# Probabilities times context values of two sequences in one product of full width, with separate instruction orders for the opening and the closing step

## The reference, cut to what matters

```python
def _L0_xattn_ref(Q, K, V, mask, Wq, Wk, Wv, Wo):
    B, S, E = Q.shape                 # 64, 64, 128
    H, Dk = (N_HEAD, D_K)             # 16, 8
    q = (Q @ Wq.T).reshape(B, S, H, Dk).transpose(0, 2, 1, 3)
    k = (K @ Wk.T).reshape(B, S, H, Dk).transpose(0, 2, 1, 3)
    v = (V @ Wv.T).reshape(B, S, H, Dk).transpose(0, 2, 1, 3)
    scores = jnp.einsum('bhqd,bhkd->bhqk', q, k) / jnp.sqrt(jnp.float32(Dk))
    attn = jax.nn.softmax(scores, axis=-1)
    ctx = jnp.einsum('bhqk,bhkd->bhqd', attn, v)
    ctx = ctx.transpose(0, 2, 1, 3).reshape(B, S, E)
    return ctx @ Wo.T
...
    x = x + _L0_attn_ref(_layernorm(x, axis=-1), ...)
    x = x + _L0_xattn_ref(_layernorm(x, axis=-1), ctx_1024, ctx_1024, mask_1_bf0, ...)
    x = x + _L0_ffn_ref(_layernorm(x, axis=-1), ...)
```

## Time and profile before

| | us |
|---|---|
| median of 3 runs | 347.01 |
| lowest, highest | 342.46, 348.94 |
| the profiled execution, its time | 346.9 |
| the profiled execution, span of its instructions | 345.1 |
| TensorE busy (share of the span) | 298.0 (86%) |
| TensorE weight loads busy | 214.0 (62%) |
| VectorE busy | 238.8 (69%) |
| ScalarE busy | 238.0 (69%) |
| GpSimd busy | 168.9 (49%) |

### The profile page before, as it was taken

How to read it: one execution, slowest core, us unless ns; L and a number is a source line. 1 busy time by engine, 2 the same in 40 slices (tenths; PEclk the granted TensorE clock), 3 DMA queues, 4 the chain that set the end, 5 groups by cost and what they waited for, 6 DMA issues and landing times.

```text
span 345.1 us, 9523 instructions
## 1 busy us (share of the span) xinstructions
PE 298.0 (86%) x3666; PEld 214.0 (62%) x3666; DVE 238.8 (69%) x549; ACT 238.0 (69%) x399; POOL 168.9 (49%) x210
## 2 busy tenths in 40 slices
PE   6546886999999999999999999999989988889851
PEld 6343776755866586658665866586658645745640
DVE  3764286686788788878887878787875585334546
ACT  6692744589958995899589958995898476216602
POOL 5359129225655396539653964375437531230220
PEclk9995589899999999999999999999999999659995
DMA  3901001100210011002200020012001100100011
GB/s 91 264 19 31 20 0 32 48 0 8 66 41 3 7 50 25 3 6 61 75 2 8 22 53 2 9 42 63 1 8 48 26 3 2 30 2 2 2 30 30
DMA packets 15948, 10.64 MB, mean 31 GB/s; under 512 B 2848, under 2 KB 14112, under 8 KB 15904
## 3 DMA queue, kind: packets, MB, share of 16 engines
q1 hardware_dynamic: 15648, 9.91, 10.7%
q10 hardware_dynamic: 256, 0.13, 0.2%
HBM read 4.79 MB, written 2.10 MB: 20 GB/s over the span
## 4 chain that ended last, share of the span: by engine, by line
PE 60%; ACT 14%; DVE 12%; issue 8%; ACTq 2%; SPq 2%; DMA 1%; POOL 1%; POOLq 0%; DVEq 0%
PE AT L675 10%; PE S L748 7%; PE PT L781 6%; PE PB L800 4%; PE PA L692 4%; DVE at L1380 3%; ACT pr L1118 3%; DVE nmax L1432 3%; PE S L761 3%; PE PB L813 2%; PE PA L708 2%; ACT prT L1123 2%; ACT L1089 2%; ACT L1044 2%; PE PT L580 2%
## 5 line engine op out<-in xcount | busy, mean ns | idle before, releaser
L1432 DVE TENSOR_REDUCE nmax<-S 128x16 bf16<-128x1024 f32 x30 | 36.7, 1223 | 14.9 <-PE S L748 14.9
L675 PE MATMUL AT<-q_bd,kc 128*64 128x128 f32 x512 | 36.4, 301 | 8.4 <-DVE at L1380 4.3
L800 PEld LDWEIGHTS PB<-v_x,prT 128*64 128x64 f32 x960 | 32.3, 139 | 18.0 <-ACT prT L1123 13.2
L675 PEld LDWEIGHTS AT<-q_bd,kc 128*64 128x64 f32 x512 | 32.3, 152 | 17.2 <-issue 15.1
L1123 ACT COPY prT<-PT 128x512 f32<-128x512 f32 x60 | 34.8, 580 | 11.6 <-PE PT L781 9.6
L781 PE MATMUL PT<-ident,pr 128*128 128x128 f32 x240 | 38.3, 282 | 2.5 <-ACT pr L1118 1.3
L1008 ACT ACTIVATE k_bd<-S,k_rows 128x512 f32<-128x512 f32 x64 | 39.7, 691 | 0.7 <-DVE k_rows L1541 0.7
L781 PEld LDWEIGHTS PT<-ident,pr 128*128 128x128 f32 x240 | 26.0, 140 | 22.6 <-issue 11.6
L1118 ACT ACTIVATE pr<-S,rs 128x1024 f32<-128x1024 f32 x30 | 33.4, 1115 | 9.0 <-PE S L761 9.0
L800 PE MATMUL PB<-v_x,prT 128*64 128x18 f32 x960 | 36.9, 214 | 2.9 <-ACT prT L1123 2.9
L453 POOL TENSOR_TENSOR kc<-ke,e_r 128x512 f32<-128x512 f32 x32 | 36.0, 1143 | 0.6
(11 more groups left out here) (170 smaller groups left out, 681.9 us busy)
## 6 DMA issues: line engine op xcount, KB each, us to landing
cT<-in_ctxT SPq DMA_DIRECT2D x8, 256.0 KB, 3.4
v_bd<-vt SPq DMA_DIRECT2D x32, 64.0 KB, 2.1
out<-yout SPq DMA_DIRECT2D x8, 256.0 KB, 2.2
q_bd<-qs SPq DMA_DIRECT2D x112, 8.0 KB
x_all<-in_x SPq DMA_DIRECT2D x2, 256.0 KB, 3.4
q_bd<-qs ACTq DMA_DIRECT2D x16, 8.0 KB
wv_s<-in_wv SPq DMA_DIRECT2D x1, 64.0 KB, 2.0
wg_s<-in_wg SPq DMA_DIRECT2D x1, 64.0 KB, 1.9
```

Source lines behind the costliest of these rows:

```text
L675: last = nc.tensor.matmul(AT[L * w:L * w + L, c * NB * CH:(c + 1) * NB * CH], kc_m[:, i, c, :], q_bdv[:, :, L * i + CH * c:L * i + CH * c ...
L800: last = nc.tensor.matmul(dst[L * half:L * half + L, 2 * VC * p:2 * VC * p + 2 * VC], prT_v[:, p, L * half:L * half + L], v_xv[:, g % 2, 2 ...
L1432: nc.vector.tensor_reduce(nmax[:, XH * (i % 2):XH * (i % 2) + XH], cut(s_buf(g, i), XH, L), AX.X, ALU.max, negate=True).then_inc(s_max, 1)
```

## The change

The change has two parts.

The product. `x_values` now takes all 128 columns of a block of `prT` as weights, and the values of both sequences of the tile, 2 x 18 columns, as the moving side. Every token is thus multiplied with the values of its own sequence and with those of the other one. `cx` is twice as large (`x` = 0 or 1 says with whose values). `b_weigh` takes the sums of the first part alone, since the ones are the same in both, and multiplies both parts. `x_out` no longer transposes with a transposition: for each tile and each sequence it is a product with 128 columns of `cx` as weights and 64 columns of the identity moving, which transposes and takes, of the part x, only the tokens of sequence x.

The orders. Step 0 and step 6 have lists of their own (`opening`, `closing`), `step` serves 1 to 5, and the lists of all engines are written in another order, SP's too. `keep_awake` gets more places: in `first` 14 parts before the first scores of cross attention, where there were 9, three inside `closing`, one at the start of `last` as before, three before the last transposition, where there were two. In the last group they wait for `s_og`, for they write to PA0.

```diff
@@
-        cx, cxT, x2 = sb("cx", GT), sb("cxT", GT), sb("x2", GT)
+        cx, cxT, x2 = sb("cx", 2 * GT), sb("cxT", GT), sb("x2", GT)
+        cx_v = cut(cx, TPG, 2, E)
...
@@
-        def run(first, step, last):
+        def run(first, opening, step, closing, last):
 
             first()
-            for n in range(NG - 1):
+            opening()
+            for n in range(1, NG - 2):
                 step(n)
+            closing()
             last()
...
@@
                 dst = pv_buf(g, i)
+                both = dst[:, 0:2 * XH * VC].rearrange("p (x q v) -> p x q v", x=2, q=PAIRS)
                 for p in range(hp * n, hp * n + hp):
-                    for half in range(2):
-                        last = nc.tensor.matmul(dst[L * half:L * half + L, 2 * VC * p:2 * VC * p + 2 * VC],
-                                                prT_v[:, p, L * half:L * half + L], v_xv[:, g % 2, 2 * i + half, p, :],
-                                                start=True, stop=True)
+                    last = nc.tensor.matmul(both[:, :, p, :], prT_v[:, p, :], v_xv[:, g % 2, 2 * i:2 * i + 2, p, :],
+                                            start=True, stop=True)
                 last.then_inc(s_PV, 1)
 
             def x_out(g):
                 pe.wait_ge(s_cx, TPG * g + TPG)
                 pe.wait_ge(s_prT, 2 * TPG * (g + 1))
-                to_features(PT, cx).then_inc(s_CX, 1)
+                for i in range(TPG):
+                    for half in range(2):
+                        at_c = P * i + L * half
+                        last = nc.tensor.matmul(PT[:, at_c:at_c + L], cx_v[:, i, half, :],
+                                                ident[:, L * half:L * half + L], start=True, stop=True)
+                last.then_inc(s_CX, 1)
...
@@
             def keep_awake(g, part):
-                if part >= AWAKE:
+                if g == NG - 1:
+                    pe.wait_ge(s_og, NG)
+                elif part >= AWAKE:
                     pe.wait_ge(s_WC, 1)
...
@@
                 dve.wait_ge(s_PV, 2 * (TPG * g + i) + 2)
-                pv = pv_buf(g, i)[:, 0:XH * VC].rearrange("p (h v) -> p h v", h=XH)
+                pv = pv_buf(g, i)[:, 0:2 * XH * VC].rearrange("p (x h v) -> p x h v", x=2, h=XH)
                 mine = rden[:, XH * (i % 2):XH * (i % 2) + XH].unsqueeze(2)
-                nc.vector.reciprocal(mine, pv[:, :, XD:VC]).then_inc(s_rden, 1)
+                nc.vector.reciprocal(mine, pv[:, 0, :, XD:VC]).then_inc(s_rden, 1)
                 dve.wait_ge(s_rden, TPG * g + i + 1)
                 if i == 0:
                     dve.wait_ge(s_CX, g)
-                nc.vector.tensor_tensor(cx[:, E * i:E * i + E].rearrange("p (h v) -> p h v", h=XH), pv[:, :, 0:XD],
-                                        mine.to_broadcast([P, XH, XD]),
+                nc.vector.tensor_tensor(cx_v[:, i, :, :].rearrange("p x (h v) -> p x h v", h=XH), pv[:, :, :, 0:XD],
+                                        mine.unsqueeze(1).to_broadcast([P, 2, XH, XD]),
                                         ALU.mult).then_inc(s_cx, 1)
```

More of the change, by code:

```diff
@@ L321, in last @@
                 pass
-            run(first, step, last)
+            run(first, opening, step, closing, last)
             sp.wait_ge(s_out, 16 * NG)
@@ L537, in step @@
+                group_norm(b)
+                route2(c)
+                spans(a)
+                count(c)
+                products(a)
                 if has(a + 2):
                     scale_a(a + 2)
[L539 to L549, removed]
@@ L886, in first, with opening @@
                 scores(1, 1)
+                x_scores(0, 0)
+            def opening():
                 attend(1, 0, 0)
+                attend(1, 0, 1)
+                attend(1, 1, 0)
+                less_max(0, 0)
+                project_qk(2)
+                x_scores(0, 1)
+                x_attend(0, 0, 0)
+                attend(1, 1, 1)
+                less_max(0, 1)
+                project_g(2)
+                x_attend(0, 0, 1)
+                x_scores(0, 2)
+                less_max(0, 2)
+                x_values(0, 0, 0)
+                x_values(0, 0, 1)
+                project_v(2)
+                x_scores(0, 3)
+                x_attend(0, 1, 0)
+                transpose_o(1)
+                x_attend(0, 1, 1)
+                x_values(0, 1, 0)
+                aug_weights(2)
+                x_values(0, 1, 1)
+                x_attend(0, 2, 0)
+                less_max(0, 3)
+                x_attend(0, 2, 1)
+                transpose_x(3)
+                context_keys(2)
+                x_values(0, 2, 0)
+                x_values(0, 2, 1)
+                x_attend(0, 3, 0)
+                gla_out(1)
+                x_attend(0, 3, 1)
+                x_values(0, 3, 0)
+                x_values(0, 3, 1)
+                context_values(2)
+                x_out(0)
+                scores(2, 0)
+                x_out2(0)
+                queries(1)
+                scores(2, 1)
+                queries2(1)
+                attend(2, 0, 0)
             def step(n):
@@ L941, in step, with closing @@
                 x_out2(n)
[L942 to L944 removed]
+                scores(a, 0)
                 queries2(b)
[L946 to L948 removed]
+                scores(a, 1)
+                attend(a, 0, 0)
+            def closing():
+                attend(7, 0, 1)
+                x_scores(6, 0)
+                transpose_x2(5)
+                attend(7, 1, 0)
+                attend(7, 1, 1)
+                less_max(6, 0)
+                router(5)
+                ffn(5)
+                x_attend(6, 0, 0)
+                x_scores(6, 1)
+                x_attend(6, 0, 1)
+                x_values(6, 0, 0)
+                less_max(6, 1)
+                x_scores(6, 2)
+                x_attend(6, 1, 0)
+                x_values(6, 0, 1)
+                less_max(6, 2)
+                x_attend(6, 1, 1)
+                x_values(6, 1, 0)
+                x_scores(6, 3)
+                transpose_o(7)
+                x_values(6, 1, 1)
+                x_attend(6, 2, 0)
+                less_max(6, 3)
+                x_attend(6, 2, 1)
+                x_values(6, 2, 0)
+                gla_out(7)
+                x_attend(6, 3, 0)
+                x_values(6, 2, 1)
+                x_attend(6, 3, 1)
+                x_values(6, 3, 0)
+                x_values(6, 3, 1)
+                keep_awake(7, 23)
+                x_out(6)
+                keep_awake(7, 21)
+                x_out2(6)
+                queries(7)
+                keep_awake(7, 22)
+                queries2(7)
```

568 lines of the change are left out of this document (346 added, 222 removed).

## The result

The changed kernel takes 375.39 us in the median of 4 runs (373.63 to 379.92); the kernel before took 346.85 us in 4 runs beside it. The ratio is 1.085, with a 95% interval of 1.071 to 1.099: 8.5% slower. The forecast was 377 us. The profiled execution took 376.2 us, with a span of 374.5 us, 29.4 us more than before.

What follows compares the result with a forecast made beforehand. TensorE was taken to bound steps 1 to 5. Steps 0 to 5 at 4.5 us each gave 27; with 0, -0.3 and +3.4 at the ends, +30 on 346.9 made 377 us; 8-in-10 range 359 to 389 us.

Steps and rivals of the forecast that it cites:

- What a load of full width costs: TensorE weight loads: 128 columns for a product take 0.11 us, 64 columns 0.058 beside the other sequence's.
- (1): Rival: a full-width load costs 0.06 us like a transposition's, x_values costs nothing, 351 us in all; 6%.
- (2): Rival: with the cheap load, a clock held from the first scores through step 6 makes it faster, 340 us; 4%.
- (3): Rival: loads are not hidden behind products of the same rows, a step +7.2 us, about 396 us; 3%.
- (4): Rival: new orders fill TensorE's waits, 3.3 us a step, ends at low bounds, 359 us; 87% together with the forecast.
- x_values: Half a tile takes 0.89 us instead of 0.46, +0.42, 8 times a step: +3.4 us.
- x_out: Four transposes become 16 full-width instructions, 1.78 us: +1.3 us a step.
- Waits and orders in a middle step: TensorE's 0.4 us wait for prT goes; tile 2's scores wait +0.6 for tile 1's exponential.
- A middle step: Grows by 3.3 to 5.3 us, taken as 4.5; the step lasts 38 to 40 us.
- first: New orders at the start: held clock may return some 5 us, against added delays; bounds -4 and +4, taken 0.
- Step 6: Work +4.7, keep_awake +2.7, full clock worth 5.5, some 2 of waits filled: -0.3 us, bounds -5 and +7.
- last: x_values +3.4, x_out +1.3, less 0.8 for clock and 0.5 for waits: +3.4 us, bounds +1.5 and +5.

Runs made afterwards that it cites:

- e3: Changed kernel with the moving side of x_values cut from 36 to 18 columns: 407.5 us, ratio 1.178 to the kernel before.
- e8: Changed kernel with the moving side of x_values widened from 36 to 54 columns: 373.01 us, ratio 1.082 to the kernel before.
- e9: Kernel before with the new x_values alone, old orders, VectorE picking the own half in b_weigh: 356.27 us, ratio 1.036.
- e4: Changed kernel with x_out as four transposes again and VectorE picking the own half in b_weigh: 367.04 us, ratio 1.068 to the kernel before.
- e2: Changed kernel with the old x_values, x_out and b_weigh put back, new orders kept: 347.72 us, ratio 1.012 to the kernel before.
- e1: Kernel before with the new x_values, x_out and b_weigh, every list in the old order: 372.48 us, ratio 1.085.
- e7: e2 with the first half of tile 0's values and project_g ahead of tile 2's scores in middle steps: 347.64 us, ratio 1.009.
- e6: Changed kernel without the three groups of keep_awake in closing: 378.42 us, ratio 1.101 to the kernel before.
- e10: e3 with two groups of four identity products, 128 columns moving, added in steps 1 to 5: 405.36 us, ratio 1.166.
- e5: Kernel before with four more groups of keep_awake in step 6 alone: 341.97 us, ratio 0.993.
- e11: e5 with keep_awake also before x_out, x_out2 and the last transposition of the last group: 341.56 us, ratio 0.993 to the kernel before.
- e12: e11 with keep_awake also put into the waits of first: 338.18 us, ratio 0.984 to the kernel before.

## Why the prediction was right, and where two of its terms were not

- **What a load of full width costs** held: 0.111 us, measured at L830 and, whatever the moving side, in e3 and e8. With it the sign and the size. Rivals (1) and (2) have fallen, (3) too. (4) did not come about: a middle step gained 3.75 us and not 3.3, and the ends were not at their low bounds.
- **x_values**, +3.4 us a step, was too much. It measured 1.8 in the old orders (e9), and in the new ones 37.31 - 35.69 = 1.6 (e4 against e2). Two things were left out of the term. Between groups of full width there is no passage: half a tile ends after 0.81 us, not 0.89, and in the old order four passages go with the old product (14 where there were 18), six in the new one (18 where e2 has 24). I had compared 18 with 18 across both edits at once and taken the product's share as nothing. And of the 1.4 us of waits 0.8 were filled, for `prT`, the exponential and the maximum (e9 has 0.6 left), of which the prediction had counted 0.4, under waits.
- **x_out**, +1.3, measured 1.2 (e1 against e9) and 1.0 (e4 against the changed kernel).
- **Waits and orders in a middle step** were too little. I had a net +0.2 us (+0.6 - 0.4), with which the terms add up to 4.9 and not to the 4.5 that I took; no term stands for the 0.4 between them. The new order costs 0.8 with the new product (38.28 against 37.48) and 1.2 with the old one. The wait before the scores of tile 2 is there as forecast, 0.8, but e7, with the old product, shows that moving it elsewhere gains nothing: the sum of the waits stays. With the new product that sum is 1.4 us in the new order and 0.6 in the old one (e9), as much as the 0.8 us.
- **A middle step** came to +3.75 for +4.5. The product was over by 1.7 us, the orders under by 0.6 to 1.0, and the 0.4 were taken off without a reason. That the errors partly cancelled is luck.
- **Step 0** came to +6.0 for +4.5; 2.9 of it are its new order (e2).
- **first**: +1.1 for 0, in these two executions. The clock did not hold up to the scores. It was back for the second group of them alone, and `scores(1, 0)` ran at half clock as before; the first group began at 36.85 us instead of 33.77:

```profile
36.85 3.34 PE L705 MATMUL AT<-q_bd,kc 128*64 128x128 f32 x32 [1.46 <-issue]
41.67 1.97 PE L705 MATMUL AT<-q_bd,kc 128*64 128x128 f32 x32 [1.48 <-DVE at L1553]
...
60.74 3.68 PE L705 MATMUL AT<-q_bd,kc 128*64 128x128 f32 x32 [0.46 <-issue]
```

Seven experiments have the same `first` as the changed kernel (e2, e3, e4, e6, e7, e8, e10), and their step 0 begins between 63.58 and 66.58 us; with the old one (before, e1, e5, e9, e11) it begins between 65.14 and 66.66. The +1.1 is thus within what one execution differs from another, and shows no cost of the new `first`.

- **Step 6**: -0.5 for -0.3 (the terms add up to -0.1), by the mechanism given: the groups of `keep_awake` hold the clock (e6), and the product cost 4.8 us for the forecast 4.7 (against e2).
- **last**: +3.5 for +3.4, but not at every place as forecast. The feed-forward products ran at full clock, as I had it (1.16 us at 365.53, where the earlier trace rows has 1.68). In exchange `x_out`, in part, and `x_out2` ran at half clock (from 354.70 us on), which they had not before; the mean over `last` is 0.88, for 0.86 before.
- The sum of the profiled executions is 1.1 + 6.0 + 4 x 3.75 + 4.2 (step 5) - 0.5 + 3.5 = 29.3, against 30. Between the medians it is 28.5.

## What to carry to other kernels

Count a product's weight columns before its instructions: where few columns move, two loads of half width that run beside each other beat one of full width, and halving the number of instructions gains nothing. When an edit changes a product and the order around it, compare each with the other held fixed, since passages between half and full width belong to both. Useless products in waits of TensorE paid for themselves twice here, where the clock had stood at half while TensorE had work to do (step 6 in e5, `first` in e12). In the tail they gained nothing that the whole shows (e11). Before a few us at the start or the end of a program are put down to an edit, look at executions of other kernels with the same list there: step 0 began up to 4.2 us apart here (63.58 to 67.80 us).

## What the runs showed of the hardware that was not expected

The clock fell while TensorE had work. With 18 instead of 36 moving columns beside the same loads (e3), TensorE was busy 23.84 of 24.66 us and still went from 2.4 to 1.2 GHz in each of the steps 1 to 5; a change that took work away made the kernel 32 us slower (407.5 against 375.39 us). The Trainium skill, TensorE: Matmul & The Clock Gate, HAM oscillation, lays a falling clock to gaps without products; here the trace shows one where there was no gap over 0.3 us in the 3 us before. What exactly counts was not settled: step 0 of e3 kept the full clock with 18 columns as well, and e10's added products shortened the stretch at half clock in a middle step from 13.6 to 3.4 us, did not remove it, and left steps 5 and 6 longer at half clock.
